# First attention layer: VectorE compares four of the seven one-hot planes, ScalarE takes a distance in three, and every widening becomes max(0, 1 - y)

## The reference, cut to what matters

```python
def _gatv2_layer(x, src, dst, Wl, Wr, a, b):
    xl = (x @ Wl).reshape(N, H, O)
    xr = (x @ Wr).reshape(N, H, O)
    s = jax.nn.leaky_relu(xl[src] + xr[dst], NEG_SLOPE)
    e = jnp.einsum('eho,ho->eh', s, a)
    m = jax.ops.segment_max(e, dst, num_segments=N)
    ex = jnp.exp(e - m[dst])
    denom = jax.ops.segment_sum(ex, dst, num_segments=N)
    alpha = ex / (denom[dst] + 1e-16)
    out = jax.ops.segment_sum(xl[src] * alpha[:, :, None], dst, num_segments=N)
    return out.reshape(N, H * O) + b
...
x = x + gnn_three_layers(relu(layernorm(x)), edges)
x = x + gin_layer(relu(layernorm(x)), edges, edge_attr_16)
```

## Time and profile before

| | |
|---|---|
| median of 3 runs | 6389.84 us (6387.47 to 6390.85) |
| the profiled execution's own time | 6388.7 us |
| its span, first to last instruction | 6386.9 us |
| busy over the span | PE 91%, PEld 77%, DVE 78%, ACT 70%, POOL 73% |
| first layer's turns, 1000 to 1500 us | PE 469.4, DVE 482.3, ACT 396.8, POOL 383.2 us busy of 500; DMA engines 75%, 239 GB/s |
| second layer's turns, 1800 to 3100 us | PE 1262.1, DVE 1182.8, ACT 1044.7, POOL 983.3 us busy of 1300; DMA engines 56%, 175 GB/s |

### The profile page before, as it was taken

How to read it: one execution, slowest core, us unless ns; L and a number is a source line. 1 busy time by engine, 2 the same in 40 slices (tenths; PEclk the granted TensorE clock), 3 DMA queues, 4 the chain that set the end, 5 groups by cost and what they waited for, 6 DMA issues and landing times.

```text
span 6386.9 us, 100693 instructions
## 1 busy us (share of the span) xinstructions
PE 5833.5 (91%) x26550; PEld 4898.7 (77%) x26550; DVE 5002.2 (78%) x7592; ACT 4458.6 (70%) x6151; POOL 4694.1 (73%) x4884
## 2 busy tenths in 40 slices
PE   2899999999789999999969999999986999999996
PEld 1677777778578888888858888888865888888884
DVE  8699999999769999999958999999985444444443
ACT  1577777777558888888837888888874666666663
POOL 3777777777677777777767777777767777777775
PEclk9999999999799999999969999999997999999996
DMA  9677777777445555555535555555543444444442
GB/s 390 226 243 237 239 241 238 240 239 240 148 139 177 176 177 178 178 179 179 180 96 165 177 176 177 176 177 180 179 158 87 149 145 148 149 144 146 144 146 59
DMA packets 452762, 1153.09 MB, mean 181 GB/s; under 512 B 158556, under 2 KB 224592, under 8 KB 416636
## 3 DMA queue, kind: packets, MB, share of 16 engines
q1 hardware_dynamic: 281384, 927.55, 40.2%
q0 software_dynamic: 156944, 173.32, 14.8%
q10 hardware_dynamic: 14404, 51.92, 2.1%
HBM read 754.01 MB, written 398.35 MB: 180 GB/s over the span
## 4 chain that ended last, share of the span: by engine, by line
POOL 49%; issue 20%; PE 11%; DVE 9%; DMA 5%; ACT 3%; SPq 2%; POOLq 0%; DVEq 0%; ACTq 0%
POOL sb_xl L530 45%; PE pG L619 10%; DMA sb_xl<-xl_table,sb_idx 4%; POOL sb_hot_f L530 3%; DVE pG L1194 1%; POOL marks L534 1%; SPq L353 1%; DVE sb_e_in L1260 1%; DVE sb_lr L1258 1%; DVE sb_s L1256 1%; ACT sb_v_in L740 1%; DVE sb_s_run L1236 1%; DMA sb_idx<-src_edges 1%; DVE sb_v_g L1290 1%; PE pB L696 1%
## 5 line engine op out<-in xcount | busy, mean ns | idle before, releaser
L619 PE MATMUL pG<-sb_xl_parts,sb_hot 128*128 128x476 f32 (+1 forms) x25074 | 5524.0, 379 | 230.6 <-ACT sb_xl L740 122.2
L619 PEld LDWEIGHTS pG<-sb_xl_parts,sb_hot 128*128 128x128 f32 x25074 | 4694.1, 189 | 1056.6 <-issue 435.4
L530 POOL DMA_INDIRECT sb_xl<-xl_table,sb_idx x4481 | 4298.0, 959 | 1382.1 <-issue 1357.2
L740 ACT ACTIVATE sb_hot<-sb_wide 128x1792 fp32r<-128x1792 bf16 (+1 forms) x796 | 1486.3, 1881 | 276.2 <-DMA sb_wide<-hots 251.6
L1194 DVE COPY_PREDICATED pG<-sb_pick_turn,pG 128x272 f32<-128x272 int32 (+9 forms) x2388 | 1112.1, 466 | 552.6 <-PE pG L619 449.8
L1236 DVE TENSOR_TENSOR_SCAN sb_s_run<-pB,sb_v_in 128x272 f32<-128x272 f32 (+3 forms) x1470 | 1096.3, 773 | 221.7 <-ACT sb_v_in L968 221.2
L740 ACT ACTIVATE sb_turn_out<-sb_s_run 128x1088 f32<-128x1088 f32 (+3 forms) x395 | 833.9, 2111 | 11.3 <-DVE sb_s_run L1236 11.0
L1233 DVE TENSOR_TENSOR_SCAN pB<-sb_same_c,pB 128x1024 f32<-128x1024 f32 x294 | 672.1, 2286 | 0.1
L740 ACT ACTIVATE sb_v_in<-sb_v_g 128x1024 f32<-128x1024 f32 x291 | 600.9, 2065 | 0.0
L740 ACT ACTIVATE sb_xl<-pG 128x136 f32<-128x136 f32 (+4 forms) x838 | 251.7, 303 | 485.7 <-DVE pG L1194 398.3
L1256 DVE TENSOR_TENSOR sb_s<-sb_xl,pB 128x1024 f32<-128x1024 f32 x294 | 356.0, 1211 | 169.6 <-DMA sb_xl<-xl_table,sb_idx 166.6
(11 more groups left out here) (237 smaller groups left out, 2321.7 us busy)
## 6 DMA issues: line engine op xcount, KB each, us to landing
state_rows<-sb_turn_out SPq DMA_DIRECT2D x294, 576.0 KB
sb_wide<-hots SPq DMA_DIRECT2D x149, 1120.0 KB
sb_mark<-marks SPq DMA_DIRECT2D x294, 512.0 KB
sb_wide<-hots SPq DMA_DIRECT2D x149, 896.0 KB
sb_xl<-xl_table,sb_idx POOLq DMA_INDIRECT x4481
sb_wide<-codes SPq DMA_DIRECT2D x50, 1120.0 KB
hots<-sb_wide SPq DMA_DIRECT2D x50, 1120.0 KB, 4.3
marks<-sb_hot_f SPq DMA_DIRECT2D x32, 1568.0 KB
```

Source lines behind the costliest of these rows:

```text
L530: return pool.indirect_dma_start(out=dst, out_offset=None, in_=table, in_offset=bass.IndirectOffsetOnAxis(ap=index, axis=0))
L619: product = pe.matmul(pG[:, bank + a - lo, 0:GB * n], hot[k][:, m, a * P:(a + 1) * P], rows[:, :, 0:n], start=(m == 0 and part == 0), stop ...
L740: return act.activation(out, in_, ACT.Copy)
```

## The change

VectorE now compares only planes 0 to 3, with `not_equal` in place of `is_equal`: planes 0 and 1 in one instruction between stage 1 and `begin_xr`, planes 2 and 3 in a second one where the whole compare was. ScalarE takes planes 4 to 6 with one activation, the absolute value of code minus the partition's number (`distances`), between `rows_copied` q = 1 and the wait for the sums. Both leave y = 0 where the one-hot is 1 and y of 1 or more elsewhere, so each widening, in all four layers, becomes max(0, 1 - y), a Relu with scale -1 and bias 1. SyncE's store of the matrix, and in the first layer the widenings, wait for the distances too (`s_far`).

```diff
+BUILD_FIRST = 2
+BUILD_LAST = 4
...
+            sp.dma_start(minus_code_no[:, :], t["minus_code_no"]).then_inc(s_minus, 16)
...
                 sp.wait_ge(s_hot[k], built)
                 sp.sem_inc(s_passed, 1)
+                sp.wait_ge(s_far[k], built)
+                sp.sem_inc(s_passed, 1)
                 store_hot(step, k)
...
+            def distances(built, k):
+
+                act.wait_ge(s_code[k], (built + 1) * 16)
+                act.sem_inc(s_passed, 1)
+                sl = slice(BUILD_LAST * EC[k], HOT[k])
+                act.activation(staged[k].rearrange("p m e -> p (m e)")[:, sl], staged_code[k][:, sl], ACT.Abs,
+                               bias=minus_code_no[:, 0:1], scale=1.0).then_inc(s_far[k], 1)
+
-            def widen(ready, filled, used, k, q, n=TW):
+            def widen(ready, filled, used, k, q, n=TW, fresh=False):
...
+                if fresh:
+                    act.wait_ge(s_far[k], filled)
+                    act.sem_inc(s_passed, 1)
...
-                copy(hot[k][:, :, lo * P:hi * P], staged[k][:, :, lo * P:hi * P]).then_inc(s_wide[q], 1)
+                act.activation(hot[k][:, :, lo * P:hi * P], staged[k][:, :, lo * P:hi * P], ACT.Relu, bias=one_col[:, 0:1], scale=-1.0).then_inc(s_wide[q], 1)
...
                     rows_copied(selected, use + k, 1, 1 - k)
+                if fresh and ahead >= 3:
+                    distances(i + (2 + k), 1 - k)
                 act.wait_ge(s_sums, turn_all + 1)
...
-            def build_one_hot(built, k):
+            def not_here(k, lo, hi):
+
+                sl = slice(lo * EC[k], hi * EC[k])
+                return ts(staged[k].rearrange("p m e -> p (m e)")[:, sl], staged_code[k][:, sl], code_no[:, 0:1], None, ALU.not_equal)
+
+            def codes_here(built, k):
 
                 dve.wait_ge(s_code[k], (built + 1) * 16)
                 dve.sem_inc(s_passed, 1)
-                ts(staged[k].rearrange("p m e -> p (m e)"), staged_code[k], code_no[:, 0:1], None, ALU.is_equal).then_inc(s_hot[k], 1)
...
                     select_stage(1 - k, 0, 1).then_inc(s_pick, 1)
+                    if build:
+                        codes_here(i + (2 + k), 1 - k)
+                        not_here(1 - k, 0, BUILD_FIRST)
                     begin_xr(turn_all + 1, bass.ds(turn + 1, 1), 1 - k, l * (TURNS - 1) + turn + 1)
...
                     select_stage(1 - k, 0, 2).then_inc(s_sel[0], 1)
                     if build:
-                        build_one_hot(i + (2 + k), 1 - k)
+                        not_here(1 - k, BUILD_FIRST, BUILD_LAST).then_inc(s_hot[1 - k], 1)
                     scan_xr(turn_all + 1)
```

More of the change, by code:

```diff
@@ L148, in build @@
         code_no = sb("code_no", [P, 1])
+        minus_code_no = sb("minus_code_no", [P, 1])
+        one_col = sb("one_col", [P, 1])
         pick = sb("pick", [P, 3, STEP_PAIRS * PAIR])
@@ L277, in build @@
         s_code, s_hot, s_wide = two("code_in"), two("one_hot_built"), two("one_hot_widened")
+        s_minus, s_far = sem("minus_codes_in"), two("distances_taken")
         s_hot_out, s_hot_in = two("one_hot_stored"), two("one_hot_in")
@@ L449, in _ @@
                 sp.wait_ge(s_hot[k], 1)
+                sp.wait_ge(s_far[k], 1)
                 store_hot(k, k)
@@ L794, in widen_first @@
                 if fresh:
-                    widen(s_hot, i + (k + 3), used, 1 - k, 0)
+                    widen(s_hot, i + (k + 3), used, 1 - k, 0, fresh=True)
                 else:
@@ L802, in widen_second @@
                 if fresh:
-                    widen(s_hot, i + 3, used, k, 1)
+                    widen(s_hot, i + 3, used, k, 1, fresh=True)
                 else:
@@ L900, in widen_step @@
                     if fresh:
-                        widen(s_hot, step // 2 + 1, max(step - 1, 0), step % 2, q)
+                        widen(s_hot, step // 2 + 1, max(step - 1, 0), step % 2, q, fresh=True)
                     else:
@@ L906, in attention_layer @@
                     act.wait_ge(s_filled, 16 * (2 + J // B))
+                    act.wait_ge(s_minus, 16)
+                    for k in range(2):
+                        distances(0, k)
                 for q in range(2):
@@ L919, in attention_layer @@
                         turn_masks(1, step)
+                        if fresh:
+                            distances(1, step)
                         for q in range(2):
                             widen_step(step + 2, q)
+                    elif fresh:
+                        distances(2, 0)
                 act.wait_ge(s_start, l + 1)
@@ L1062, in _ @@
             dve.memset(neg_col[:, :], NEG)
+            dve.memset(one_col[:, :], 1.0)
             dve.memset(rs[:], 0.0)
@@ L1330, in attention_layer @@
                     if build:
-                        build_one_hot(1 + step // 2, step % 2)
+                        codes_here(1 + step // 2, step % 2)
+                        not_here(step % 2, 0, BUILD_LAST).then_inc(s_hot[step % 2], 1)
                 dve.wait_ge(s_xr_first, (l + 1) * 16)
@@ L1414, in _ @@
             for k in range(2):
-                build_one_hot(0, k)
+                codes_here(0, k)
+                not_here(k, 0, BUILD_LAST).then_inc(s_hot[k], 1)
             prologue_steps = steps[0]
@@ L1595 @@
         "code_no": (np.arange(P, dtype=np.float32) * GB).reshape(P, 1),
+        "minus_code_no": (np.arange(P, dtype=np.float32) * -GB).reshape(P, 1),
         "identity": np.eye(P, dtype=np.float32),
```

## The result

| | before | after |
|---|---|---|
| median | 6390.09 us (6387.47 to 6390.85, 4 runs) | 6621.38 us (6618.06 to 6622.19, 4 runs) |
| ratio | | 1.0362, 95% interval 1.035 to 1.0375 |
| span of the profiled execution | 6386.9 us | 6618.4 us |

The change costs 231 us. The direction and the mechanism are those of the prediction (slower, 0.87); the size is not: 130 us were forecast and the range ended at 6600. In three later measurements, on three chips, the kernel before itself took 8671 to 8690 us, and the traces taken there show TensorE in waits that the profile calls "remote"; what was measured beside it is marked, and compares with nothing else.

A forecast was written before the change was run, and what follows sets the result against it. GpSimd's gathers, held up by VectorE's compare, were taken to bound the kernel; the change would close a loop through SyncE's store and load: 93 x 1.37 = 127 us, plus about 3, on 6388.7 gives 6519, median 6520 us; range 6435 to 6600.

The forecast's parts named there:

- Which loop, and that it decides: First layer: codes landed, first piece, ScalarE's work, distances, store, load, codes landed; sets the turn, +1.37 us, chance 0.82.
- The turn forecast of 16.34 us: First layer's loop: 8.74 + 7.6 in even turns, 8.14 + 8.2 in odd, against 14.97 us before.
- Codes landed to store, 8.74 and 8.14 us: Loop's part from codes' landing through first piece, ScalarE's work and distances to store issue, even and odd turn.
- The 796 dearer widenings: ScalarE's widenings, all layers: Relu for copy taken at no cost; uncovered, 0.05 us more each would be 40 us.
- Store issued to codes landed, 7.6 and 8.2 us: Loop's DMA part on SyncE: store 4.3 and 3.8 us plus load's moving time 3.3 and 4.4, start-up hidden.
- the "lull": Load behind the store: a pause of 0.8 to 1.0 us before it moves would give 17.3 us turns, 6609 us.
- GpSimd's hold-up, 0.1 us a turn left: First layer's gathers: VectorE's compare delays GpSimd about 0.6 us a turn; the shorter pieces leave 0.1.
- Rival 2: First layer: load lands in time, GpSimd sets the pace, turns of 14.48 us, -48 us, 6342 us; chance 0.08.
- SyncE's later items: SyncE's indices, state rows and marks: late by 2 us but with a turn or more of air.
- Rivals 3 and 4: First layer: 3, part of both, 6355 to 6402 us, chance 0.05; 4, distances cost like turning copy, 6690 us, 0.05.

The follow-up runs named there:

- the wait without the work: The kernel before, with the store of the matrix also waiting for `rows_copied` q = 1 and no distances added: 6464.8 us, ratio 1.0111.
- less work on it: The changed kernel with VectorE comparing six planes and ScalarE taking the distance in one: 6547.4 us, ratio 1.0239.
- the first experiment: The changed kernel with SyncE issuing the load of the codes ahead of the store of the matrix: 6366.4 us against 6393.0, ratio 0.9958.

## Why the prediction was right and where it was wrong

**Which loop, and that it decides.** Right. Loading first opens it and the loss is gone; the wait without the work closes it (+71.8 us); less work on it shortens the turn by 0.8 of what it saves. The turn forecast of 16.34 us came out at 17.4.

**Codes landed to store, 8.74 and 8.14 us.** Right: 8.61 and 8.14. In it, the distances were put at 1.80 and 1.48 us and take 1.89 and 1.57, 0.1 us too little each; the first piece was put at 0.38 and 0.31, and 0.46 and 0.40 us pass until `begin_xr` starts. What made this good is the copy of q = 1, put at 0.28 us ahead of the distances, which begin 0.16 us after it (1225.66 and 1225.82), and in the even turn ScalarE's stretch before it, 5.17 us for 5.29. That is partly luck. The missing 0.1 us of the distances is most likely the bias, an operand of one number for each partition, though no run takes the bias alone away: the widenings, which got one too, went from 1694 and 2440 ns to 1787 and 2541. The Trainium skill has this (ScalarE: Activation LUTs, "What ACT_TABLE_LOAD costs"): about 280 ns and 0.833 ns an element with such a bias, and about 93 ns for each such operand. The trace agrees: by that rule an estimate for 1,920 and 1,536 elements is 1.88 and 1.56 us. I had fitted the rows of a copy without a bias and stopped there. The 796 dearer widenings cost nothing, as forecast: 400 gathers in 500 us of the second layer.

**Store issued to codes landed, 7.6 and 8.2 us.** This is the step that failed: "I let the load's start-up vanish behind the store and add only its moving time." Measured 9.07 and 8.99 us, 1.13 us more in the mean. The first half of the sentence holds, as far as the means go. In the run with nothing behind the load, the codes landed 8.65 and 8.44 us after the store's issue (0.77 + 7.98 - 0.10 and 0.70 + 7.84 - 0.10) and thus 3.45 and 4.04 us after the store's own landing; forecast were 3.3 and 4.4. Mis-sized was the store, and what is queued behind the load, 1,096 KB, the sum had at nothing:

- the store lands later with a load right behind it, 5.2 and 4.4 us for the 4.3 and 3.8 of rows 7: +0.9 and +0.6;
- the load lands later with indices, state rows and marks right behind it: +0.42 and +0.55;
- the load's moving time: +0.15 and -0.36.

The mean of the three is 0.75 + 0.49 - 0.10 = 1.13 us, and with 0.07 less ahead of the store it is 1.06 us a turn: 93 x 1.06 = 99 us, and 6520 + 99 = 6619, measured 6621.4. I had the rows for a bound, the "lull" that would give 17.3 us and 6609, and put the range's end below it.

Why a transfer gets longer by what is queued behind it is shown in part only: the engines move 0.45 MB of the followers before the load has landed (2.51 MB against 2.06). For the store it is less: in the run with nothing behind the load the queue moved 1.32 MB in the 5.2 us to the landing of a store of 1,120 KB (1.15 MB), so 0.17 MB of the load. That these bytes make the whole delay is not shown. The Trainium skill says of the rings of one issuing engine that descriptors are taken in order, but that a later one may finish its write before an earlier one (DMA: Bandwidth & Descriptors, "Queues, rings and completion order"). That both would be in flight together fits the store that lands 0.8 to 1.0 us later, and the 1.9 us a turn that queueing saves over waiting for the store's landing; no run here looks into a ring.

**GpSimd's hold-up, 0.1 us a turn left.** Right: in the run with the load first a gather takes 374.46 / 392 = 955 ns, 998 before, against the 0.94 us of an undisturbed one in rows 3. The closed loop makes it worthless.

**Rival 2, the load in time and 14.48 us a turn.** It didn't come about, but the run with the load first shows what it would have given: 14.72 us and -27 us, not -48. GpSimd waits 8.1 us in 500 for its indices there, one of SyncE's later items, and 1.5 us for VectorE: 0.28 us a turn above its own pace. Rivals 3 and 4 fell, by the first experiment and by the 1.89 us.

**SyncE's later items "have a turn or more of air".** Wrong, without effect on the time: GpSimd waits 51.0 us in 500 for its indices. Inside a closed loop this only moves idle time, which is argued; with the loop open it cost the 8.1 us above.

## What to carry to other kernels

When a wait is added to an instruction that issues a DMA, look at what the same queue issues next, and whose input that is: here the store could wait, and the load behind it could not, and swapping two lines turned +3.6% into -0.4%. When a gap between issue and landing becomes part of a loop, take its length from a place where the queue is as full as it will be; a landing that was measured with a free queue behind it was 0.6 to 0.9 us too short here. And a long compare that holds up GpSimd can be eased by cutting it in two (998 to 976 ns a gather here, 24 us in all), before its work is given to another engine.

## What the runs showed of the hardware that was not expected

- A store of 1,120 KB landed 4.2 us after its issue with nothing behind it and 5.2 us with a load right behind; one of 896 KB landed after 3.6 and 4.4 us.
- A load of 896 KB took from issue to landing or use 5.4 us with a store 2.9 us later, 6.75 us with the store 0.7 us later, 6.5 us after a landed store with 1,096 KB of indices, state rows and marks behind it, and 8.4 us behind a store and ahead of them. 1,120 KB took practically the same as 896 KB in the last three, though it moves a quarter more.
